# The order of a cross-attention kernel's last round, and two skipped PSUM banks

## The reference

```python
# layer 0: 16 heads of 64
q, k, v = layernorm(x) @ Wq * scale, *split(media @ Wkv)
x = x + tanh(attn_gate) * (softmax(where(mask, q @ k.T, -inf)) @ v) @ Wo
x = x + tanh(ff_gate) * (gelu(layernorm(x) @ W1) @ W2)
# layer 1: one head, keys and values are the projected memory
mp = memory @ W_mem.T
ctx = softmax(x @ mp.T / sqrt(256)) @ mp
gate = sigmoid(concat(x, ctx) @ W_gate + b_gate)
fused = x + gate * ctx
out = fused * rsqrt(mean(fused ** 2) + 1e-6) * norm_w
```

## Time and profile before

| | us |
|---|---|
| median of 3 runs | 878.66 (878.57 to 879.61) |
| the profiled execution | 878.46 |
| its span, first to last instruction | 876.7 |
| TensorE busy | 834.0 (95%) |
| VectorE busy | 587.7 (67%) |
| ScalarE busy | 463.7 (53%) |
| GpSimd busy | 399.2 (46%) |

### The profile page before, as it was taken

How to read it: one execution, slowest core, us unless ns; L and a number is a source line. 1 busy time by engine, 2 the same in 40 slices (tenths; PEclk the granted TensorE clock), 3 DMA queues, 4 the chain that set the end, 5 groups by cost and what they waited for, 6 DMA issues and landing times.

```text
span 876.7 us, 18163 instructions
## 1 busy us (share of the span) xinstructions
PE 834.0 (95%) x7751; PEld 699.1 (80%) x7751; DVE 587.7 (67%) x964; ACT 463.7 (53%) x726; POOL 399.2 (46%) x185
## 2 busy tenths in 40 slices
PE   4999999999999999999999999999999999998984
PEld 3787878888888888888887888888888778887773
DVE  6857788867567788675678886756787612134574
ACT  4755656657356666563565665645554441225261
POOL 2445565655625656565356565553566550000000
PEclk8999999999999999999999999999999999999998
DMA  9100001000000000000000000000001600000200
GB/s 280 25 2 1 1 5 36 1 1 1 1 1 1 15 25 1 1 2 1 2 1 1 1 1 1 2 1 1 1 1 36 180 1 1 1 1 1 76 19 30
DMA packets 20559, 16.80 MB, mean 19 GB/s; under 512 B 1008, under 2 KB 19456, under 8 KB 20480
## 3 DMA queue, kind: packets, MB, share of 16 engines
q1 hardware_dynamic: 20192, 15.38, 6.0%
q10 hardware_dynamic: 288, 0.27, 0.1%
HBM read 14.59 MB, written 1.05 MB: 18 GB/s over the span
## 4 chain that ended last, share of the span: by engine, by line
PE 79%; DVE 12%; ACT 5%; POOL 1%; issue 1%; DMA 1%; ACTq 0%; POOLq 0%; DVEq 0%
PE psum L1257 21%; PE psum L1271 17%; PE psum L343 13%; PE psum L1226 7%; PE psum L1182 4%; PE psum L1286 3%; PE psum L1034 3%; PE psum L1048 3%; PE psum L1121 3%; DVE mx L886 2%; DVE k_lo L875 2%; DVE ot L916 1%; PE psum L1277 1%; ACT k_hi L600 1%; POOL acc L443 1%
## 5 line engine op out<-in xcount | busy, mean ns | idle before, releaser
L443 POOL TENSOR_TENSOR acc<-acc,ring 128x1024 f32<-128x1024 f32 x128 | 306.8, 2397 | 18.7 <-POOL acc L438 0.5
L886 DVE TENSOR_REDUCE mx<-psum 128x2 f32<-128x800 f32 (+2 forms) x256 | 245.5, 989 | 88.9 <-PE psum L1226 81.1
L623 ACT ACTIVATE ring<-psum 128x1024 f32<-128x1024 f32 x192 | 196.9, 1027 | 67.3 <-PE psum L1257 60.9
L438 POOL TENSOR_TENSOR acc<-ring 128x1024 f32<-128x1024 f32 x32 | 76.6, 2394 | 276.7 <-ACT ring L623 276.7
L1271 PE MATMUL psum<-ring,v 128*64 128x256 f32 (+1 forms) x1664 | 186.7, 381 | 1.7
L1271 PEld LDWEIGHTS psum<-ring,v 128*64 128x64 f32 (+1 forms) x1664 | 116.8, 137 | 60.9 <-DVE k_lo L875 3.8
L1257 PE MATMUL psum<-nm,maskrow 64*128 64x256 f32 (+1 forms) x832 | 124.3, 295 | 0.6 <-ACT ring L623 0.6
L1257 PE MATMUL psum<-q_hi,k_hi 64*128 64x256 f32 (+1 forms) x832 | 117.5, 278 | 0.0
L1257 PE MATMUL psum<-q_lo,k_hi 64*128 64x256 f32 (+1 forms) x832 | 117.2, 277 | 0.0
L1257 PE MATMUL psum<-q_hi,k_lo 64*128 64x256 f32 (+1 forms) x832 | 117.1, 277 | 0.0
L615 ACT COPY od<-psum 128x512 f32<-128x512 f32 x32 | 18.8, 587 | 167.7 <-PE psum L1277 167.7
(11 more groups left out here) (149 smaller groups left out, 1347.3 us busy)
## 6 DMA issues: line engine op xcount, KB each, us to landing
nat<-in_ctx_dram SPq DMA_DIRECT2D x7, 768.0 KB
w<-in_L_xattn_W_dram SPq DMA_DIRECT2D x2, 1024.0 KB, 8.9
wo<-in_L_xattn_Wo_dram SPq DMA_DIRECT2D x1, 1024.0 KB, 10.3
out_dram<-t_res SPq DMA_DIRECT2D x8, 128.0 KB, 1.8
mask<-in_mask_BxS_bk_dram SPq DMA_DIRECT2D x4, 200.1 KB, 7.3
nat<-in_ctx_dram SPq DMA_DIRECT2D x2, 384.0 KB, 7.1
ring<-in_L_xattn_Wkv_dram SPq DMA_DIRECT2D x2, 384.0 KB, 6.8
wq<-in_L_xattn_Wq_dram SPq DMA_DIRECT2D x1, 768.0 KB, 7.2
```

Source lines behind the costliest of these rows:

```text
L438: nc.gpsimd.tensor_tensor(acc[:, :, :, :], ring[:, 0, :, :, :], ring[:, 1, :, :, :], ALU.add)\
L443: nc.gpsimd.tensor_tensor(acc[:, :, :, :], acc[:, :, :, :], ring[:, g, :, :, :], ALU.add)\
L623: nc.scalar.activation(ring[:, g, :, :, :], score_set[m % 2].rearrange("p (h i q) -> p h i q", h=2, i=2), ACT.Exp).then_inc(S["p_ready"], 1)
L886: nc.vector.tensor_reduce(mx[:, t, :, c], pair[:, :, 0:min(c1, KEYS) - c0], axis=AX.X, op=ALU.max).then_inc(S["m_max"], 1)
```

## The change

Two parts. In `side_banks` two banks are skipped ahead of ("G", 6), so that G.6 and what comes after it in BODY's last phase sit two banks further; M.3.0 then follows K.3.3 and R.2, M.3.1 follows A.1 and V.1.6, G.6 follows M.10.7, K.11.0 follows O.0 (in FIRST M.10.6), and K.11.1 follows M.10.7.

In the last round TensorE runs the token halves of the gates of both lanes ahead of the weighted media, and lane 1's weighted media in two parts of 128 tokens, with lane 0's context and lane 1's first context between. The mean square, the root and the wait of the result go by tile, in both rounds; the semaphores `u_psum`, `u_ready`, `ssq_ready` and `rms_ready` count tiles. ScalarE and VectorE take the last round's tiles in an order written out by hand. Round 0's order on TensorE and ScalarE is as before.

```diff
@@ -122,6 +122,8 @@
         for item in BODY:
             if item[0] == "M":
                 n += n % 2
+            if item == ("G", PAIRS - 2):
+                n += 2
             if item[0] in USES_BANK:
                 table[item] = n % ABANKS
                 n += 2 if item[0] == "M" else 1
@@ -405,7 +407,7 @@
 
             for it in range(ROUNDS):
                 for lane in range(LANES):
-                    need(sp, ("u_psum", lane), it, 1, 0)
+                    need(sp, ("u_psum", lane), it, QT, 0)
                     sp.dma_start(nats[lane][:, 0:KT - 1, :], media_full[it * LANES + lane, :, :, :])\
                         .then_inc(S["media_in", lane], 16)
                     sp.dma_start(nats[lane][0:TAIL, KT - 1, :], media_tail[it * LANES + lane, :, :])\
@@ -428,6 +430,11 @@
 
             def reciprocal_root(lane, done):
                 nc.gpsimd.tensor_tensor(rstd[:, lane, :], var[:, lane, :], mhalf[:, 0, :], ALU.pow).then_inc(S[done], 1)
+
+            def rms_root(it, lane, t):
+                need(pool, ("ssq_ready", lane), it, QT, t + 1)
+                nc.gpsimd.tensor_tensor(rstd[:, lane, t:t + 1], var[:, lane, t:t + 1], mhalf[:, 0, t:t + 1], ALU.pow)\
+                    .then_inc(S["rms_ready", lane], 1)
 
             def sums(b, next_batch):
 
@@ -470,8 +477,8 @@
             reciprocal_root(BATCH - 1, "ff_rstd")
             for it in range(ROUNDS):
                 for lane in range(LANES):
-                    need(pool, ("ssq_ready", lane), it, 1, 1)
-                    reciprocal_root(lane, ("rms_ready", lane))
+                    for t in range(QT):
+                        rms_root(it, lane, t)
 
         @block.scalar
         def _(act):
@@ -504,9 +511,9 @@
                 nc.scalar.activation(gms_hi[i % LANES][:, :], gm_bank[i][:, 0:TOK], ACT.Copy, scale=L1_SCALE)\
                     .then_inc(S["gm_hi_ready"], 1)
 
-            def tanh(it, lane):
-
-                for t in range(QT):
+            def tanh(it, lane, tiles=range(QT)):
+
+                for t in tiles:
                     need(act, ("ctx_ready", lane), it, QT, t + 1)
                     nc.scalar.activation(gate_s[lane][:, t, :], gate_s[lane][:, t, :],
                                          ACT.Tanh, scale=0.5).then_inc(S["gate_ready", lane], 1)
@@ -528,14 +535,15 @@
                                    lane_bank[lane][u % 4][0:r, 0:w * TOK].rearrange("p (t q) -> p t q", t=w))\
                         .then_inc(S["pt_act", lane], 1)
 
-            def u_in(it, lane):
-
-                need(act, ("u_psum", lane), it, 1, 1)
-                nc.scalar.copy(uts[lane][:, :], lane_bank[lane][3][:, 0:TOK]).then_inc(S["u_ready", lane], 1)
-
-            def finish(it, lane):
-
-                for t in range(QT):
+            def u_in(it, lane, tiles=(0, 1)):
+
+                c0, c1 = tiles[0] * P, (tiles[-1] + 1) * P
+                need(act, ("u_psum", lane), it, QT, tiles[-1] + 1)
+                nc.scalar.copy(uts[lane][:, c0:c1], lane_bank[lane][3][:, c0:c1]).then_inc(S["u_ready", lane], len(tiles))
+
+            def finish(it, lane, tiles=range(QT)):
+
+                for t in tiles:
                     need(act, ("fused_ready", lane), it, QT, t + 1)
                     nc.scalar.activation(squares[lane][:, t, :], fuseds[lane][:, t, :], ACT.Square,
                                          accum_out=l1sum[lane][:, t:t + 1]).then_inc(S["square_ready", lane], 1)
@@ -666,16 +674,22 @@
                 for lane in range(LANES):
                     if it:
                         finish(it - 1, lane)
-                for lane in range(LANES):
-                    if it < ROUNDS - 1:
-                        x2_turned(LANES * (it + 1) + lane)
-                    u_in(it, lane)
                 if it < ROUNDS - 1:
                     for lane in range(LANES):
+                        x2_turned(LANES * (it + 1) + lane)
+                        u_in(it, lane)
+                    for lane in range(LANES):
                         memory_hi(LANES * (it + 1) + lane)
-            for lane in range(LANES):
-                tanh(ROUNDS - 1, lane)
-                finish(ROUNDS - 1, lane)
+            last = ROUNDS - 1
+            u_in(last, 0)
+            u_in(last, 1, (0,))
+            tanh(last, 0)
+            tanh(last, 1, (0,))
+            finish(last, 0)
+            u_in(last, 1, (1,))
+            finish(last, 1, (0,))
+            tanh(last, 1, (1,))
+            finish(last, 1, (1,))
 
         @block.vector
         def _(dve):
@@ -756,10 +770,10 @@
                                           lane_bank[lane][u % 4].rearrange("p (t q) -> p t q", t=2))\
                         .then_inc(S["pt_dve", lane], 1)
 
-            def context(it, lane):
+            def context(it, lane, tiles=range(QT)):
 
                 need(dve, ("gx_ready", lane), it, 1, 1)
-                for t in range(QT):
+                for t in tiles:
                     need(dve, ("ctx_psum", lane), it, QT, t + 1)
                     bank = lane_bank[lane][2 + t]
                     nc.vector.tensor_scalar(cxs[lane][:, t, :], bank[:, 0:DIM], l1rec[lane][:, t:t + 1], None, ALU.mult)
@@ -778,9 +792,9 @@
                                         bgate[:, :].unsqueeze(1).broadcast_to([P, QT, DIM]), ALU.add)\
                     .then_inc(S["gx_ready", lane], 1)
 
-            def fuse(it, lane):
-
-                for t in range(QT):
+            def fuse(it, lane, tiles=range(QT)):
+
+                for t in tiles:
                     need(dve, ("gate_ready", lane), it, QT, t + 1)
                     tail_step(nc.vector.scalar_tensor_tensor(fuseds[lane][:, t, :], gate_s[lane][:, t, :], 1.0,
                                                              cxs[lane][:, t, :], ALU.add, ALU.mult))
@@ -788,17 +802,18 @@
                                                    xs[:, it * LANES + lane, t, :], ALU.mult, ALU.add)\
                         .then_inc(S["fused_ready", lane], 1)
 
-            def mean_square(it, lane):
-
-                need(dve, ("square_ready", lane), it, QT, QT)
-                nc.vector.tensor_scalar(var[:, lane, :], l1sum[lane][:, :], 1.0 / DIM, RMS_EPS, ALU.mult, ALU.add)\
-                    .then_inc(S["ssq_ready", lane], 1)
-
-            def result(it, lane):
-
-                need(dve, ("rms_ready", lane), it, 1, 1)
+            def mean_square(it, lane, tiles=range(QT)):
+
+                for t in tiles:
+                    need(dve, ("square_ready", lane), it, QT, t + 1)
+                    nc.vector.tensor_scalar(var[:, lane, t:t + 1], l1sum[lane][:, t:t + 1], 1.0 / DIM, RMS_EPS,
+                                            ALU.mult, ALU.add).then_inc(S["ssq_ready", lane], 1)
+
+            def result(it, lane, tiles=range(QT)):
+
                 need(dve, ("out_stored", lane), it, 16 * QT, 0)
-                for t in range(QT):
+                for t in tiles:
+                    need(dve, ("rms_ready", lane), it, QT, t + 1)
                     nc.vector.scalar_tensor_tensor(ress[lane][:, t, :], fuseds[lane][:, t, :],
                                                    rstd[:, lane, t:t + 1], normw[:, :],
                                                    ALU.mult, ALU.mult).then_inc(S["out_ready", lane], 1)
@@ -975,12 +990,23 @@
                     if it < ROUNDS - 1:
                         memory_lo(LANES * (it + 1) + lane)
                     gate_of_tokens(it, lane)
-                for lane in range(LANES):
-                    context(it, lane)
-            for lane in range(LANES):
-                fuse(ROUNDS - 1, lane)
-                mean_square(ROUNDS - 1, lane)
-                result(ROUNDS - 1, lane)
+                if it < ROUNDS - 1:
+                    for lane in range(LANES):
+                        context(it, lane)
+            last = ROUNDS - 1
+            context(last, 0)
+            context(last, 1, (0,))
+            fuse(last, 0)
+            fuse(last, 1, (0,))
+            mean_square(last, 0)
+            result(last, 0, (0,))
+            context(last, 1, (1,))
+            mean_square(last, 1, (0,))
+            result(last, 0, (1,))
+            fuse(last, 1, (1,))
+            result(last, 1, (0,))
+            mean_square(last, 1, (1,))
+            result(last, 1, (1,))
 
         @block.tensor
         def _(pe):
@@ -1114,13 +1140,14 @@
                                                        p1s[lane][:, q, t * P:t * P + r], ident[:, :])
                     last.then_inc(S["pt_psum", lane], 1)
 
-            def weighted_media(it, lane):
-
-                for t in range(KT):
-                    r = rows_of(t)
-                    last = mm(lane_bank[lane][3][:, 0:TOK], nats[lane][0:r, t, :], pts[lane][0:r, t, :],
-                              start=(t == 0), stop=(t == KT - 1))
-                last.then_inc(S["u_psum", lane], 1)
+            def weighted_media(it, lane, parts=((0, TOK),)):
+
```

(37 more changed lines are left out.)

## The result

The changed kernel takes 872.39 us (median of 6 runs, 872.16 to 872.56) against 878.75 for the kernel before (6 runs, 878.39 to 879.61): a ratio of 0.9928, with a 95% interval of 0.9918 to 0.9937. It is faster by 0.72%, where 872.8 was forecast, and within the range. The profiled execution took 872.35 us, with a span of 870.5.

What follows compares the result with a forecast made beforehand. TensorE, busy 95% of the span, left gains only in its idle gaps or the tail, where VectorE's serial order ends last. 876.7 - 2.25 (skip) - 3.44 (tail) = 871.0, plus 1.76 gives 872.8 us; range 871.0 to 876.2.

Steps and rivals of the forecast that it cites:

- The skip: At three changes of batch, M.3.0 starts 0.53 us after D and not 1.28: 0.75 each, 2.25 us in all.
- move to M.3.1: Rival at the changes of batch: the wait for `od` only moves, or VectorE's maxima hold TensorE back: 875.1 us; chance 0.13.
- the 0.9 of idle named among the signs: Sign expected in FIRST: 0.9 us of idle ahead of G.6.
- 0.73 at the one out of FIRST: At the change out of FIRST, 0.73 us gained, eaten by a loss of 0.71 at G.6: net nothing.
- TensorE in the tail: Last round: gates first, lane 1's media in halves of 2.99 us, 0.115 an instruction; last context readable at 866.53.
- the rival of the weight loads: Tail: weight loads of 0.19 us set the spacing of lane 1's half matmuls: 876.6 us; chance 0.07.
- VectorE in the tail: Last round in VectorE's new order: the last result ends at 870.95 where it ended at 874.39; tail gain 3.44 us.
- the two bounds: Time of a one-column root on GpSimd, two on the tail's path: 0.35 to 0.69 us, taken as 0.69.
- The rival of the reordered tail: Tail: if lane 0's tiles don't fit ahead of the last context, 3.44 us becomes 1.6: 874.6 us; chance 0.06.
- The gates: Last round: gates start at 847.16 in place of the weighted media; bias additions no longer stand between matmuls and contexts.
- The roots by tile: Round 0: four roots in a row, at most 1.4 us later; tail: two one-column roots on the path, 0.69 each.
- The slower rival: Tail: granted clock falls to 1.2 GHz, 9.4 us of matmuls take twice as long: 882.2 us; chance 0.04.

Runs made afterwards that it cites:

- kernel with lane 1 whole: The changed kernel with lane 1's weighted media whole again and its two contexts after lane 0's: 874.87 us, ratio 0.9957 to the kernel before.
- the one with the old readers: The changed kernel with TensorE's new order and roots by tile, but ScalarE's and VectorE's last round in the order of before: 875.69 us.
- the second kernel on them: The changed kernel with the gates' token halves after lane 1's first half, and lane 1's wait for its copies ahead of lane 1's media: 872.53 us.
- the second try of the tail's order: The changed kernel with FIRST's old banks, tanh wait moved, lane 1's second half ahead of its contexts, VectorE's result and mean square moved earlier: 870.58 us.

## Why the prediction was right, and where it was not

**The skip: right.** M.3.0 comes 0.53 after D and not 1.28, the forecast 0.75; from mark to mark the three changes gave 2.1 us together, where 2.25 was forecast, and the skip alone took 876.33 us, where 876.5 was expected. The wait did not move to M.3.1, which starts at 253.23, half a microsecond after the copy's end (252.12 + 0.59).

**FIRST: 0.2 us short.** It was forecast as net nothing. From the first D to the second it lost 0.73 (21.47 against 20.74), as the sum had it at G.6 (0.71; the 0.9 of idle named among the signs was 0.65), and from there to the third regained 0.51 (22.01 against 22.52), not 0.73. The step that failed is "0.73 at the one out of FIRST": VectorE's wait for the tanh of the gates had been hidden behind the wait for `od`, and no list of before shows it. FIRST with its own banks and the wait moved removed both losses.

**TensorE in the tail: right.** The halves were taken at 0.115 an instruction. The second one took 3.06 us for 26, less the 0.27 of the last one 2.79 for 25: 0.112, with weight loads of 0.19 each. The first context started 8.52 after the first weighted media, where 8.60 was forecast. That settles the rival of the weight loads, which needed 0.19, and with it the estimate from the Trainium skill, "TensorE: Matmul & The Clock Gate", section "Back-to-back issue gap": the half costs 0.52 of a whole one here (0.112 of 0.216), not 0.83.

**VectorE in the tail: right in its course, 0.3 short in size.** The forecast put the last result 23.79 after the start of the gates; it was 23.46. The root is the largest part: one of one column took 0.54 on the path and not 0.69, between the two bounds. From its start to the result that it releases that saved only 0.08, twice: 0.66 (863.12 to 863.78, and 867.22 to 867.88) where the forecast had 0.74. The first context came 0.07 sooner after the gates than forecast (13.11 against 13.18); the last 0.1 is spread over the short steps. The copy of the second half took 0.24 and not 0.37, but that did not shorten the path by as much: the last context's data were there at about 864.06 (862.93 + 1.13), while VectorE was at lane 0's result, and it took them next, at 864.18.

```profile
L436 POOL TENSOR_TENSOR rstd<-var,mhalf x8: 539/546/710, 848.9 to 867.2; 128x1 f32<-128x1 f32 x8
```

**The rival of the reordered tail: wrong, and worth its place.** It said that the gain hangs on VectorE's order alone. The kernel with lane 1 whole has that order and loses 2.7 us of the 3.8; the one with the old readers has TensorE's order and loses 3.5. Neither gives the whole gain without the other.

**The gates: costed rightly, for a reason that was only half there.** The prediction gave their move no gain of its own, and the second kernel on them agrees. It did not see that without the move the change would have cost 0.66, because a wait for lane 1 had slid ahead of lane 0's media.

**The roots by tile** were costed at their length alone. Their use is the order that they allow: 0.74 in the new order, by a run, and some 1.1 in the old, read from traces.

**The slower rival** did not come: the granted clock stayed in the top tenth to the end, and the halves ran at 0.112 an instruction.

**The number** was met in part by luck. The sum took 5.69 us off the profiled execution, and by the marks the change took 5.7 off: the tail was 0.33 better than forecast, and FIRST and the changes of batch together 0.3 worse. Of the 0.4 by which the profiled execution lies below the forecast, 0.33 is the earlier first D, which no step of the prediction is about.

## What to carry to other kernels

Where a shared bank's first use after a boundary waits for the last reader of the work before it, turn the banks, here by two. It cost nothing at the three boundaries with the usual order; look at the one boundary that has another order, and at the waits that the old one was hiding. At the end of a kernel split the last producer only as far as it brings the reader's first work forward, and then write the reader's order out so that short steps that start another engine (a mean square before its root) stand ahead of long ones that nobody waits for. When a producer is reordered, read which of its waits now stand ahead of work that does not need them.

## What was not expected of the hardware

A root of one column on GpSimd took 0.54 to 0.71 us (median 0.55), one of two columns 0.70 in the same place: half the work, four fifths of the time. The 0.71 was always the root of lane 1's first tile, in every kernel with the changed kernel's order of roots by tile (865.19 here) and in the second try of the tail's order; why was not tried.
